# The first and the last steps of a layer's software pipeline, written out with an order of their own on every engine

## The reference, cut to what matters

```python
xn = _layernorm(x)
# s: 16 heads of width 8; blocks of 64 keys, the maximum carried from block to block
scores = einsum('bhqd,bhkd->bhqk', Q, K_blk) * SCALE
m_new = maximum(m, scores.max(-1)); corr = exp(m - m_new)
chunk_sum = exp(scores - m_new).sum(-1)
l_new = chunk_sum * corr + chunk_sum
out_new = out * corr + einsum('bhqk,bhkd->bhqd', exp(scores - m_new), V_blk)
s = (out / l) @ out_w.T + out_b
# f: per batch, 4 of 16 heads of width 64 are chosen from the mean of xn @ Wr + br
dist = softmax(mean(xn @ Wr + br, axis=1)); top_vals, top_idx = top_k(dist, 4)
Qk, Kk, Vk = chosen heads of the projections * gates
f = softmax(Qk Kk^T / 8) Vk @ Wo + bo
x = x + s * silu(f)
```

## Time and profile before

| | us |
|---|---|
| median of three runs | 1105.07 |
| lowest and highest of them | 1103.41, 1105.41 |
| the profiled execution | 1104.67 |
| its span, first to last instruction | 1102.9 |
| of it, last stage (from the first `transpose_x`) | 360.7 to 1102.9 |

### The profile page before, as it was taken

How to read it: one execution, slowest core, us unless ns; L and a number is a source line. 1 busy time by engine, 2 the same in 40 slices (tenths; PEclk the granted TensorE clock), 3 DMA queues, 4 the chain that set the end, 5 groups by cost and what they waited for, 6 DMA issues and landing times.

```text
span 1102.9 us, 28968 instructions
## 1 busy us (share of the span) xinstructions
PE 978.7 (89%) x9146; PEld 681.3 (62%) x9146; DVE 926.9 (84%) x2016; ACT 814.8 (74%) x1984; POOL 721.8 (65%) x1035
## 2 busy tenths in 40 slices
PE   2576537999998589999999999999999999999996
PEld 2455427999997356666666666666666666666653
DVE  6769997999998479888888888888888888888782
ACT  2456425877775358888888888888888888888884
POOL 4476777778888466666676667666766676666431
PEclk9766668999999679999999999999999999999998
DMA  9511115555553433233323332333333333333310
GB/s 256 126 37 40 40 37 146 166 163 160 164 155 113 99 80 97 77 85 94 95 77 86 99 89 76 92 95 88 77 98 87 88 79 97 96 78 76 91 42 17
DMA packets 157438, 106.42 MB, mean 96 GB/s; under 512 B 72745, under 2 KB 137449, under 8 KB 157161
## 3 DMA queue, kind: packets, MB, share of 16 engines
q1 hardware_dynamic: 153192, 96.05, 33.4%
q0 software_dynamic: 4096, 8.53, 2.6%
HBM read 72.95 MB, written 31.47 MB: 95 GB/s over the span
## 4 chain that ended last, share of the span: by engine, by line
PE 59%; issue 4%; POOL 2%; DVE 1%; SPq 1%; DMA 0%; ACT 0%; POOLq 0%
PE PS L1973 10%; PE PS L1928 6%; PE PS L2021 6%; PE PS L1950 6%; PE PS L2076 5%; PE PS L2051 5%; PE PS L2094 5%; PE PS L2036 4%; PE PS L1906 3%; PE PS L2104 3%; PE PS L1989 2%; PE PS L2008 2%; PE PS L1894 1%; DVE bm L1599 1%; PE PS L2102 1%
## 5 line engine op out<-in xcount | busy, mean ns | idle before, releaser
L1599 DVE TENSOR_REDUCE bm<-PS 128x16 f32<-128x1024 f32 x256 | 311.6, 1217 | 74.2 <-PE PS L1928 72.7
L1818 ACT ACTIVATE PT<-PS 128x1024 f32<-128x1024 f32 x256 | 261.7, 1024 | 59.7 <-PE PS L1950 59.6
L1483 POOL TENSOR_TENSOR Pr<-Pr,linv 128x512 f32<-128x512 f32 x128 | 131.7, 1040 | 65.1 <-DVE linv L1626 63.3
L1973 PE MATMUL PS<-PT,rows 128*32 128x256 f32 x2048 | 136.4, 384 | 0.1
L1791 ACT ACTIVATE Pr<-PS,nmf 128x256 f32<-128x256 f32 x256 | 117.0, 470 | 4.6 <-DVE nmf L1619 4.6
L1928 PE MATMUL PS<-KS,QS 48*128 48x256 bf16 x1024 | 101.3, 276 | 7.7 <-DVE bm L1599 5.3
L1950 PE MATMUL PS<-QS,KS 51*128 51x256 bf16 x1024 | 99.6, 272 | 3.4 <-ACT PT L1818 1.6
L474 POOL DMA_INDIRECT xs_dram<-rows,slot x64 | 65.6, 1025 | 38.8 <-DVEq L703 21.1
L1008 PE MATMUL PS<-S,wmix 128*128 128x256 f32 x192 | 69.0, 446 | 19.3 <-DVE diff L731 18.3
L1973 PEld LDWEIGHTS PS<-PT,rows 128*32 128x32 f32 x2048 | 57.2, 109 | 46.3 <-issue 18.3
L1619 DVE TENSOR_REDUCE nmf<-PS 128x4 f32<-128x1024 f32 x64 | 78.0, 1219 | 7.8 <-PE PS L2051 7.8
(11 more groups left out here) (251 smaller groups left out, 2473.0 us busy)
## 6 DMA issues: line engine op xcount, KB each, us to landing
up<-in_up_w SPq DMA_DIRECT2D x72, 256.0 KB, 3.2
wsel<-in_qkv_w SPq DMA_DIRECT2D x128, 96.0 KB, 2.5
parts_dram<-parts SPq DMA_DIRECT2D x32, 384.0 KB, 2.6
QS<-parts_dram SPq DMA_DIRECT2D x64, 96.0 KB
KS<-parts_dram SPq DMA_DIRECT2D x64, 96.0 KB
xs_dram<-zero_t SPq DMA_DIRECT2D x1, 4752.0 KB, 26.6
xs_t<-xs_dram SPq DMA_DIRECT2D x24, 198.0 KB, 2.8
ys_dram<-ys_t SPq DMA_DIRECT2D x24, 192.0 KB
```

Of the source, the lines that this page charges most:

```text
L1483: pool.tensor_tensor(Pr[i][:, qt, :, :], Pr[i][:, qt, :, :], linv[:, i, qt, :].unsqueeze(2).broadcast_to([P, 2, SEQ]), ALU.mult).then_inc( ...
L1599: dve.tensor_reduce(bm[:, i // 2, :, 2 * (i % 2):2 * (i % 2) + 2, :].rearrange("p q r b -> p r q b"), bS.rearrange("p (r q b k) -> p r q b ...
L1818: act.activation(PT[i % 4][:, :, :], shifted_bank(t, i).rearrange("p (r k) -> p r k", r=2), ACT.Exp).then_inc(s_exp, 1)
L1973: last = pe.matmul(b_values_out[u][j * VC:(j + 1) * VC, 0:SEQ], V2[t % NQ][:, kt, :, :].rearrange("p h c -> p (h c)")[:, at:at + VC], PT[( ...
```

## The change

For each of the five engines the first steps and the last steps are taken out of the loop and written as a list of calls. The middle steps (s = 5 or 6 to 29) keep the order of before, now without the `if`s. The pieces themselves and their number are the same. In the lists some pieces come earlier or later than before: at the start `transpose_x(1)` goes ahead of `project_qk(0)`, `transpose_x(2)` and `logits(2)` go in between the score blocks of batch 0, `head_scores` of the second half of batches 0 and 1 go ahead of the score blocks, and `head_v(0)` goes behind `scores(0, 1)`; on SP `load_biases(1)` goes ahead of `store_parts(1)` and `load_heads(2)` ahead of `store_max(0)`. At the end `head_scores(B - 1, 1)` goes ahead of `scores(B - 1, 0)`, the score blocks of batch B-1 are interleaved more tightly, ahead of the shifted ones of batch B-2, and `transpose_o(B - 1, 0)` goes ahead of the last `values`.

On PE the waits that order pieces which share a bank are also rewritten: where an operation waited for two or three semaphores, it mostly waits for one, chosen by t. Cut to its core, in this order of engines: SP, POOL, DVE, ACT, PE.

```diff
-            for s in range(B + 5):
+                load_max(s - 3)
+                load_heads(s - 1)
+                store_parts(s - 1)
+                load_biases(s - 1)
+                store_out(s - 5)
+                load_qk(s - 1)
+                store_max(s - 2)
+            load_heads(0)
+            store_parts(0)
+            load_biases(0)
+            load_qk(0)
+            load_heads(1)
+            load_biases(1)
+            store_parts(1)
+            load_qk(1)
+            load_heads(2)
+            store_max(0)
+            load_max(0)
+            load_biases(2)
+            store_parts(2)
+            load_qk(2)
+            store_max(1)
+            load_max(1)
+            load_heads(3)
+            store_parts(3)
+            load_biases(3)
+            load_qk(3)
...
+            load_qk(B - 1)
+            store_out(B - 6)
+            store_max(B - 2)
+            load_max(B - 2)
+            store_out(B - 5)
+            store_out(B - 4)
+            store_max(B - 1)
+            load_max(B - 1)
+            store_out(B - 3)
+            store_out(B - 2)
+            store_out(B - 1)
...
+            gather(2)
+            split_a(0)
+            split_b(0)
+            minus_top(0)
+            scale_rwkv(2)
+            minus_inverse(0)
+            residual(2)
+            gather(3)
+            head_biases(0)
+            inverse_std(2)
+            ln_apply(2)
+            minus_top(1)
...
+            minus_top(2)
+            head_norm(1, 0)
+            inverse_std(3)
+            head_norm(1, 1)
+            split_a(2)
+            ln_apply(3)
+            minus_inverse(2)
+            split_b(2)
...
+            head_qk_first(0)
+            head_max(0, 0)
+            head_max(0, 1)
+            qk_rest(1)
+            head_sum_inverse(0, 0)
+            block_max(0, 0)
+            block_max(0, 1)
+            block_max(0, 2)
+            gated(3)
+            route_b(1)
+            route_lg(2)
+            block_max(0, 3)
+            route_c(1)
+            block_max(0, 4)
+            route_max(2)
+            head_sum_inverse(0, 1)
+            block_max(0, 5)
+            head_qk_first(1)
+            block_max(0, 6)
+            route_idx(2)
+            block_max(0, 7)
+            row_max(0)
+            head_pt(0, 2)
+            head_max(1, 0)
...
+            head_max(B - 1, 1)
+            block_max(B - 1, 0)
+            block_max(B - 1, 1)
+            head_sum_inverse(B - 1, 0)
+            block_max(B - 1, 2)
+            block_max(B - 1, 3)
+            block_max(B - 1, 4)
+            block_max(B - 1, 5)
+            head_sum_inverse(B - 1, 1)
+            block_max(B - 1, 6)
+            block_max(B - 1, 7)
+            row_max(B - 1)
...
+            xT_copy(0)
+            xT_copy(1)
+            qk_copy(0)
+            z_tanh(2)
+            probs(0)
+            gate_exps(0)
+            head_qk_second(0)
+            qk_copy(1)
+            head_exp(0, 0)
+            z_tanh(3)
+            xT_copy(2)
+            v_copy(0)
+            head_v(0)
+            probs(1)
+            gate_exps(1)
+            head_exp(0, 1)
+            head_qk_second(1)
+            head_pt(0, 0)
+            head_pt(0, 1)
+            mT_copy(0)
...
+            exp_scores(B - 2, 7)
+            exp_scores(B - 1, 0)
+            head_ot(B - 1, 1)
+            exp_scores(B - 1, 1)
+            exp_scores(B - 1, 2)
+            correction(B - 1)
+            ot_copy(B - 2, 1)
+            exp_scores(B - 1, 3)
+            exp_scores(B - 1, 4)
+            routed_tanh(B - 1)
+            exp_scores(B - 1, 5)
+            ot_copy(B - 1, 0)
+            exp_scores(B - 1, 6)
+            attnT_copy(B - 2)
+            exp_scores(B - 1, 7)
+            ot_copy(B - 1, 1)
+            attnT_copy(B - 1)
         @block.tensor
...
             def transpose_x(t):
                 pe.wait_ge(s_xn1, t + 1)
-                after(pe, s_at, t - 3)
-                if t >= B - 29:
+                if t in (1, 2):
+                    after(pe, s_lg, t)
+                elif t == 3:
                     after(pe, s_g2, t - 2)
-                if t >= B - 31:
-                    after(pe, s_lg, t)
+                else:
...
                 pe.wait_ge(s_at, t + 1)
-                pe.wait_ge(s_lg, min(t + 5, B))
-                if t >= B - 4:
+                if t in (B - 4, B - 2, B - 1):
                     pe.wait_ge(s_at, t + 1)
+                elif t == B - 3:
+                    pe.wait_ge(s_otf, 2 * min(t + 2, B - 1) + 1)
+                else:
+                    pe.wait_ge(s_lg, min(t + 5, B))
...
+            transpose_x(0)
+            logits(0)
+            transpose_x(1)
+            project_qk(0)
+            logits(1)
+            head_qk(0, 0)
+            head_qk(0, 1)
+            head_scores(0, 0)
+            project_qk(1)
+            head_scores(0, 1)
+            scores(0, 0)
+            transpose_x(2)
+            scores(0, 1)
+            head_v(0)
+            scores(0, 2)
+            logits(2)
+            scores(0, 3)
+            head_qk(1, 1)
+            scores(0, 4)
+            head_qk(1, 0)
+            scores(0, 5)
+            scores(0, 6)
+            head_pt(0, 0)
+            head_pt(0, 1)
+            scores(0, 7)
+            head_pt(0, 2)
+            head_pt(0, 3)
+            head_scores(1, 0)
+            head_scores(1, 1)
+            transpose_max(0)
+            project_qk(2)
+            head_v(1)
+            scores(1, 0)
...
+            head_scores(B - 1, 1)
+            scores(B - 1, 0)
+            head_v(B - 1)
+            scores(B - 1, 1)
+            head_out(B - 2, 0)
+            scores(B - 1, 2)
+            transpose_o(B - 3, 0)
+            head_out(B - 2, 1)
+            scores(B - 1, 3)
+            shifted_scores(B - 2, 0)
+            values(B - 3, 2)
+            scores(B - 1, 4)
+            values(B - 3, 3)
+            scores(B - 1, 5)
+            shifted_scores(B - 2, 1)
+            transpose_o(B - 3, 1)
+            head_pt(B - 1, 0)
+            scores(B - 1, 6)
+            shifted_scores(B - 2, 2)
+            head_pt(B - 1, 1)
+            scores(B - 1, 7)
+            routed_out(B - 2)
+            shifted_scores(B - 2, 3)
+            head_pt(B - 1, 2)
...
+            shifted_scores(B - 1, 0)
+            head_out(B - 1, 1)
+            shifted_scores(B - 1, 1)
+            values(B - 2, 3)
+            shifted_scores(B - 1, 2)
+            values(B - 1, 0)
+            shifted_scores(B - 1, 3)
+            routed_out(B - 1)
+            shifted_scores(B - 1, 4)
+            values(B - 1, 1)
+            shifted_scores(B - 1, 5)
+            transpose_o(B - 2, 1)
+            shifted_scores(B - 1, 6)
+            transpose_o(B - 1, 0)
+            transpose_attn(B - 2)
+            shifted_scores(B - 1, 7)
+            values(B - 1, 2)
+            values(B - 1, 3)
+            project_out(B - 2)
+            transpose_o(B - 1, 1)
+            transpose_attn(B - 1)
+            project_out(B - 1)
 
 
 # ---- launch: one core; inputs and outputs as the reference has them ----

```

More of the change, by code:

```diff
@@ L1873, in step @@
[L1873 to L1883 removed]
+                mT_copy(s - 5)
+                head_exp(s - 4, 0)
+                qk_copy(s - 3)
```

1118 lines of the change are left out of this document (867 added, 251 removed).

## The result

The changed kernel takes 1110.49 us (median; 1110.01 to 1111.33), the kernel before beside it 1104.84. The ratio is 1.0057, with a 95% interval of 1.0043 to 1.0072: it is slower, by 4.8 to 8 us, and outside the forecast range, which ended at 1108.5. Timed once more among the experiments (e13) it gave 1.0043 [1.0027, 1.0058]. The profiled execution took 1110.94 us, with a span of 1109.1.

What follows compares the result with a forecast made beforehand. PE was taken to bound the kernel, full in the middle steps, so only the two ends could win. Fill -0.1, middle 0 and drain -0.75 sum to -0.85 us: 1104.2 against the median 1105.07, range 1099.8 to 1108.5.

Steps and rivals of the forecast that it cites:

- part 1: Fill up to the first score block: transpose_x(1) ahead of project_qk(0) delays it by 0.9 us, between 0.6 and 1.3.
- part 2: Eight score blocks of batch 0: -0.4 us; +0.9 at half clock all along, -3.3 at full clock.
- the credit of part 3: Stretch from scores(1, 0) to scores(2, 0): 0.6 us saved, of 1.0, as head_scores(1, 1) leaves and head_qk(2, 1) fills a hole.
- part 4: Middle steps: same pieces and order, fewer semaphore waits, 0 us, at best -3.4.
- part 5: Drain after the middle steps: -0.75 us, first shifted block of batch 31 1.3 us earlier; ends -2.7 and 0.
- part 3: Whole fill up to scores(2, 0): sum -0.1 us, with stated ends -2.9 and +1.3.
- the clock stays up: Rival at the start: denser PE work holds 2.4 GHz from the first block, fill -3.0 us, time 1101.3; chance 0.24.
- the transfer bound: KS rows for scores(2, 0): split_b(2) ends 2.7 us later, reads start 0.6 later after a 2.6 us landing, no loss.
- The rival that the dropped waits bring 3.4 us: Rival in the middle steps: dropped semaphores buy PE its 3.4 us of idle time, time 1100.8; chance 0.05.
- The parts of batch 2 come late: Rival at scores(2, 0): later split_b(2) and a 5.1 us store landing cost 2.2 us or more, time 1108.5; chance 0.18.
- Nothing moves: Rival at both ends: the same chains bind them whatever the order, time 1105.1; chance 0.08.

Runs made afterwards that it cites:

- e13: The changed kernel timed once more, unchanged, among the experiments: ratio 1.0043 to the kernel before.
- e5: Changed kernel with transpose_x(1) put back behind project_qk(0) and its copy behind qk_copy(0): 0.33% over the kernel before, 3.6 us.
- e14: Changed kernel with all repairs of order (transpose_x(1), head_exp(0, 0), both head_norm calls, last shifted block) and no useless matmuls: ratio 0.9994 to the kernel before.
- e7: Changed kernel plus 7 useless matmuls between the score blocks of batch 0: 0.8 us over the kernel before, ratio 1.0007.
- e16: e10 timed once more, unchanged: ratio 0.9983 to the kernel before.
- e9: Changed kernel with POOL's head_norm(1, 3) and head_norm(27, 3) put back behind head_biases(2) and head_biases(28): ratio 1.0014 to the kernel before.
- e11: Old start with the new end, repaired by head_norm(27, 3) put back and shifted_scores(31, 7) ahead of transpose_o(31, 0): ratio 0.9993 to the kernel before.
- e15: Old start with the 29 useless matmuls of e3 and the repaired new end of e11: ratio 0.9988 to the kernel before.
- e10: Changed kernel with all repairs of order at both ends and 23 useless matmuls ahead of and between the first score blocks: ratio 0.9979 to the kernel before.
- e12: Kernel before with POOL's head_norm(s - 3, 3) moved ahead of head_biases(s - 2) in every step: 0.47% slower, 5.2 us.
- e3: Kernel before plus 29 useless matmuls in PE's gaps from project_qk(0) to scores(0, 5): 0.06% faster, 0.7 us.
- e2: Kernel before with only the new end taken over, old start kept: 0.05% slower.
- e4: Changed kernel plus 27 useless matmuls in PE's gaps up to scores(0, 5): ratio 1.0010 to the kernel before.
- e8: New start with 27 useless matmuls, transpose_x(1) and its copy put back behind project_qk(0), and the old end; its time is not given in the text.
- e1: Kernel before with only the new start taken over, old end kept: 0.40% slower, 4.4 us.
- e6: Changed kernel plus only the 20 useless matmuls ahead of the first score block: 1.5 us over the kernel before, ratio 1.0014.

## Why the prediction was wrong

The parts forecast -0.85 us together, and the two traces differ by +5.16. Of these 6.0 us 2.6 lie in the stretch C, 0.6 in part 1, 0.3 in part 2, 0.6 in the credit of part 3, 0.9 in part 4 and 1.0 in part 5.

**Part 1 was half right.** It gave +0.9 us, with ends at 0.6 and 1.3, and measured was +1.49. `transpose_x(1)` costs 0.3 to 0.7 (e5), where 0.9 was derived. The rest comes from a list that I did not walk: in ACT's new order `head_exp(0,0)` stands behind `qk_copy(1)`, and this waits for `project_qk(1)`, which runs at half clock until 379.85. The block waits for ACT. I had written that `head_scores(0,0)` stays 4 us ahead of the block; its exponential did not. I had also not seen that the order of before has full clock ahead of the block, which the new one loses. With `head_exp(0,0)` put ahead again A is 18.57 (e14).

**Part 2 was right in sum and wrong in its reason.** It gave -0.4, measured -0.14, inside its ends; with B anywhere from 13.67 to 16.18 us in executions of this start, that nearness is in part luck. The operations cost what I had estimated for half clock (`head_v(0)` 2.93 us against 2.7). The clock came back, but not for the second `head_qk` and the pair of `head_pt`, as I let it: it came for the first `head_qk` and was gone for the second (1.13, then 2.07).

**The step that failed is the clock between part 2 and part 3.** I treated it as a question of the eight blocks, with an end of +0.9 for half clock all along, and part 3 put the cost of the stretch behind them at nothing, as if it ran at full clock as before. C had 5.94 us of PE work in the earlier trace rows, and nearly doubles if the clock is low. At half clock a `head_qk` takes 2.08 us for 1.11. The bound, an estimate of +3 us or more from these rows on a path where PE is the limit, was missing, and it is where 2.61 us went (granted clock 0.63); in the other executions of this start C is 0.5 to 2.6 us above the 6.58 of before. The rival "the clock stays up" had a chance of 0.24; "the clock stays down a little longer" had none beyond +0.9. e7 shows that filling three gaps ahead of it is enough to bring C to 6.40.

**Part 3's own credit of 0.6 us did not come either.** D is +0.03. `head_scores(1,1)` did leave the stretch, but two holes came in, since POOL's `head_norm(1,3)` was moved ahead of `head_biases(2)`. I had counted POOL's list for `split_b(2)` alone. With the holes repaired D is 20.00, which is -0.73: the credit was about right, and hidden by a collision that no row of before shows. Of the transfer bound the landing time was right and the place of `split_b(2)` was not. It ended 6.2 us later, counted from the start of the stage, where I had counted 2.7; but the reads followed the store by 2.59 us (416.53 to 419.12), as the row of 32 stores had it, and not by 5.1. So they started 3.7 us later, the block came 4.0 later, and of all kernels only e16 waits there. The ends that part 3 states, -2.9 and +1.3, are what part 2 adds to its -0.1; the ends themselves are -3.0 and +1.2.

**Part 4, no cost in the middle steps, was right** for the period: 21.95 us before and after. The +0.91 of the long stretch comes from steps written out anew. 0.63 of it lies between `scores(27,0)` and `scores(28,0)`, which take 22.58 us with the same collision (`head_norm(27,3)`), and 21.93 in e9 without it; the others give at most 0.14 each. `scores(31,0)` now waits 0.93 us for ACT, since `head_v(31)` stands behind it, but the step before it is only 0.06 us longer. The rival that the dropped waits bring 3.4 us here is refuted by the unchanged period.

**Part 5 gave -0.75, measured +0.26.** The first shifted block of batch 31 comes 23.06 us after `scores(31,0)` instead of 23.51, a gain of 0.45 where I had 1.3. From there to `values(31,2)` the new order takes 9.84 us (1088.81 to 1098.65) instead of 8.69. Part of this is `transpose_o(31,0)`, which stands ahead of the last shifted block and waits 0.89 us for DVE; with that exchange the drain takes 42.8 to 42.9 us in e11, e14, e15 and e16, and 43.3 in e10, instead of 43.3 to 43.8. What makes the rest was not tried. The old drain itself varies more than that: 43.0 to 44.5 us in the profiled executions (e12, e3). In time the new end equals the old (e2).

**The rivals.** "The parts of batch 2 come late" ended on the right side by another mechanism; its place was not where the time went. "The clock stays up" did not happen without help. The wait for the transfers that spoke against it was gone (0.67 us, for ACT), the clock was at 1.00 at the first block, and it fell all the same, to 0.50 at 386 and again at 392. With help (e4) the rival gave 1.0010, not the 1101.3 that it had been priced at, because A cost 1.5 to 1.7 us and D brought nothing. "Nothing moves" is refuted by the interval.

## What to carry to other kernels

Where PE is sparse for a while and the work behind it is dense, price the dense stretch at half clock too, as the bound of any change of order ahead of it. Here the loss was 0.5 to 2.6 us, by the execution, in a stretch that the change hardly touched. When an operation is moved on POOL, look at what DVE does at the new place, not only at who waits for the result. And when a written-out order loses, put its moves back one by one beside a version at full clock: a few exchanges and 23 useless matmuls turned +0.5% into -0.2%.

## What the runs showed that I had not expected

- A DVE operation on 64x6 elements takes 0.22 us alone, some 0.40 where it starts in the last 0.4 us of POOL's product on a 128x512 tile in SBUF (27 times in e12), and 1.05 us where it meets all of it (after); the 1.22 us maxima of DVE, which read from PSUM, are not lengthened beside it.
- Holes of 0.9 and 0.5 us on PE, in a stretch with PE busy 18.9 of 20.8 us, were followed by half clock in three profiled executions (e5, e8, e13) and by none in five others with the same holes (after, e1, e4, e6, e7). What decides it is open.
- Useless matmuls in either of two places took off most of the loss, and both together no more than one. How the first place helps the time of the kernel although it leaves C at 8.80 us was not settled: its B is the shortest of all, 12.53 us.
- One profiled execution was not typical of B: before has 16.32 us in it, and three other executions of the same start without useless matmuls have 15.2 to 15.5 (e2, e11, e12).
